# Attention and a 4-bit feed-forward pass on one core: another share-out of the decode, the weight sums and the row transfers in the down pass

## The chip, the cores and the metric

One core of one Trainium2 chip. The metric is the device time of one execution in microseconds (us), lower is better. TensorE (PE) multiplies, VectorE (DVE), ScalarE (ACT) and GpSimd (POOL) compute elementwise, SyncE (SP) and POOL issue DMAs here. Each engine runs its own instructions in program order and meets the others only at semaphores.

## The reference

Cross attention with a residual, then a gated feed-forward pass whose three weight matrices are stored as 4-bit codes with one scale for each block of 64.

```python
def reference(x, ctx, Wq, bq, Wk, bk, gate_q, gate_absmax, up_q, up_absmax, down_q, down_absmax):
    # x, ctx: (8, 256, 1024)   gate_q, up_q: (3584, 1024) int32 0..15   down_q: (1024, 3584)
    t = layernorm(x)
    Q = t @ Wq.T + bq;  K = ctx @ Wk.T + bk
    attn = softmax(Q @ K.T / sqrt(1024))
    x = x + attn @ ctx
    W = NF4_CODE[q].reshape(-1, 64) * absmax[:, None]      # for each of gate, up, down
    t = layernorm(x)
    h = silu(t @ Wg.T) * (t @ Wu.T)                        # (8, 256, 3584)
    return x + h @ Wd.T
```

## The kernel before, in words

2048 tokens go through attention, then through gate and up (a loop over slots) and through down (`DOWN_STEPS` = 98 steps). All products are made in f16 with each f32 operand split into a high and a low half (`PARTS`: high by high, high by low, low by high), and the 2 by 2 block products are made by a scheme with 7 products instead of 8 (`PRODUCTS`), which needs sums of blocks of the activations ("forms") and of the weights ("sums").

**Down pass on TensorE** (`tensor`, L1971). 7 groups of `CH_PAIRS` = 14 steps. A step m (group m // 14, c = m % 14) multiplies one pair of hidden chunks into all 8 PSUM banks, 3 matmuls of 128x512 for each bank: 24 matmuls. The banks hold a whole group; at the end of a group each bank j is emptied by VectorE (`keep_first` L2136 for group 0, `add_down` L2143 for the others) and the next group's first matmul in that bank waits for it (`s_yev`). Group 0, 1 and 2 multiply by the decoded weight quadrants 0, 1 and 2 as they are, step by step: step m needs decoded piece m. Group 3 multiplies by a difference of quadrants 3 and 0 ("sum" 0 to 13, one for each step), groups 4 to 6 by further sums 14 to 55.

**Decode.** Each of the 56 pieces of the down weights (128x512) comes from one unit: a DMA brings the codes (`load_unit`, ring of 3), ScalarE makes 10 squares (`square`, L236 and L240, into a ring of `SQ_RING` = 4 places `un.sq`), VectorE makes 5 steps (`factor`, L262 for the first, L249 for the other four, each reading one finished square and waiting for the step before it). Then ScalarE casts the high half (`piece_hi`, L287), VectorE subtracts for the low half (`piece_lo`, L294), and SP turns the piece with a DMA transpose into its place (`turn_piece`, L217; `halves` is a ring of 5). In program order ScalarE has `piece_hi` of unit v-1 behind the fifth square of unit v, VectorE has `piece_lo` of unit v-1 behind step 2 of unit v. So a unit is 11 ScalarE and 6 VectorE instructions.

**Order by plan.** `Plan` counts, before anything runs, how many decode instructions each of the two engines issues in each phase; a phase is one down step. `quota` gives at most 6 VectorE and 12 ScalarE instructions to a phase of the down pass, which comes out as one unit (6 and 11). In program order the VectorE phase m is: the last activation forms (in the first steps of group 0), `sum_lo` of the phase before, the decode instructions, `sum_of`, in two steps of groups 2, 3 and 5 `with_first` (L2129, adds group 0's kept product to the rows; 8 in all), and at c = 13 the 8 evictions. Nothing else ties these phases to TensorE's steps: an eviction comes when VectorE has gone through everything ahead of it.

**Sums** (`sum_of` L2113, L2115, L2117, `sum_hi` L2027, `sum_lo` L2123). Three VectorE operations, one ScalarE cast, one VectorE subtraction, each waiting for the one before. `SUM_AT` puts sum 0 at phase 39 and then one in each phase to 52, and sums 14 to 55 at 54 to 95.

**Queues.** SP has the transposes and, at the end, the last 8 output stores. POOL has, in each step, the stores of forms, the loads of codes due in this phase, the load of the hidden activations for step m+6 (`load_h`, L1865, waits until TensorE is done with step m), and spread over four steps each the row stores of the group before (`store_y`, c 1 to 4) and the row loads of this group (`load_y`, c 6 to 9), 256 KB each, 8 in a group.

```python
            if m - 1 in SUM_AT:
                sum_lo(SUM_AT.index(m - 1))
            streams.dve.run(DOWN_PHASE + m)
            if m in SUM_AT:
                sum_of(SUM_AT.index(m))
```

## Time and profile before

| | |
|---|---|
| median of three runs | 2038.51 us (2037.82 to 2042.64) |
| profiled execution | 2047.5 us, of it the span from first to last instruction 2045.7 us |
| mean granted TensorE clock | 0.983 |
| busy: PE, DVE, ACT, POOL | 95%, 80%, 75%, 22% |
| down pass on TensorE (L1971) | first matmul 1470.8 us, last group ends at 2041.9 us |
| its matmuls | 2352, most 379 ns long, one begun every 0.216 us |

Times in rows are microseconds from the start of the span. A busy share is over the whole span and mixes stages; TensorE is busy nearly all the time in the gate and up stage and stands still now and then in the first half of the down pass. A row of the timeline is a run of like instructions: its start, its length, how many, and in brackets how long the engine had stood still before it and what ended that. Length is from the start of the first to the end of the last; instructions of one engine overlap a little, so that the distance of two starts is less than the length of one.

### The profile page before, as it was taken

The numbers are of one execution on the slowest core, as the hardware profiler recorded it, in microseconds if no ns is written. First come the engines' busy times: TensorE is split into PE (matmuls) and PEld (weight loads), VectorE is DVE, ScalarE is ACT, GpSimd is POOL, SyncE is SP. The second block draws the span as 40 slices with busy tenths as digits, with TensorE's granted clock in tenths as the row PEclk, the third lists the DMA queues.
The fourth block names the chain that finished last, engine by engine and source line by source line (L and its number), as shares of the span: only waits on it lengthen the run. The fifth ranks groups of instructions, "written<-read, shape, count | busy, mean of one in ns | idle before, by whom it ended". The sixth has DMA issues, their size and how long they took to land.

```text
span 2045.7 us, 29927 instructions
## 1 busy us (share of the span) xinstructions
PE 1944.8 (95%) x9872; PEld 985.3 (48%) x9872; DVE 1638.0 (80%) x2716; ACT 1541.9 (75%) x2856; POOL 455.5 (22%) x688
## 2 busy tenths in 40 slices
PE   8989999989999999999999999999997996899999
PEld 3468787744444444444444444444443442334444
DVE  7758798876988898898898889888877778885763
ACT  3768876847989988988998998897999997821110
POOL 0013633630111111121111111112232332212221
PEclk9999999989999999999999999999998998999999
DMA  9012787673644655455564645556596887745544
GB/s 338 25 42 78 206 225 195 174 279 77 154 125 114 139 133 131 120 142 126 123 155 114 135 129 134 129 124 139 162 236 170 226 209 187 201 129 175 165 147 142
DMA packets 387850, 314.63 MB, mean 154 GB/s; under 512 B 327280, under 2 KB 327280, under 8 KB 385776
## 3 DMA queue, kind: packets, MB, share of 16 engines
q1 hardware_dynamic: 334544, 136.00, 30.9%
q0 software_dynamic: 51072, 176.72, 26.4%
q8 instruction: 78, 1.28, 0.3%
q14 instruction: 76, 0.62, 0.1%
q10 hardware_dynamic: 2080, 0.01, 0.1%
HBM read 154.31 MB, written 82.31 MB: 116 GB/s over the span
## 4 chain that ended last, share of the span: by engine, by line
PE 34%; ACT 29%; DVE 20%; issue 11%; DVEq 0%; POOL 0%; ACTq 0%
PE ps L1929 18%; ACT sq L240 11%; PE ps L1971 10%; ACT sq L236 9%; DVE w L249 4%; ACT halves L287 3%; DVE tail L2096 2%; PE ps L1336 2%; ACT tail L2002 2%; PE ps L1297 2%; DVE halves L294 1%; ACT tail L2017 1%; DVE tail L2062 1%; DVE ps L2052 1%; PE ps L1273 1%
## 5 line engine op out<-in xcount | busy, mean ns | idle before, releaser
L1929 PE MATMUL ps<-T,wS 128*128 128x512 f16 x4704 | 1019.9, 379 | 10.5 <-ACT ps L1986 6.3
L1929 PEld LDWEIGHTS ps<-T,wS 128*128 128x128 f16 x4704 | 458.5, 98 | 568.5 <-issue 15.4
L249 DVE SCALAR_TENSOR_TENSOR w<-sq,w 128x512 f32<-128x512 f32 x672 | 477.3, 710 | 127.8 <-ACT sq L240 115.1
L240 ACT ACTIVATE sq<-sq 128x512 f32<-128x512 f32 x1008 | 572.0, 624 | 0.0
L236 ACT ACTIVATE sq<-q 128x512 f32<-128x512 int32 x672 | 409.4, 629 | 55.5 <-DVE w L249 54.4
L1971 PE MATMUL ps<-T,tail 128*128 128x512 f16 x1584 | 351.1, 383 | 42.0 <-DVE tail L2143 20.0
L1971 PEld LDWEIGHTS ps<-T,tail 128*128 128x128 f16 x1584 | 155.3, 99 | 235.3 <-issue 40.8
L287 ACT CAST halves<-w 128x512 f16<-128x512 f32 x252 | 155.1, 616 | 79.9 <-DVE w L249 69.1
L1971 PE MATMUL ps<-T,wS 128*128 128x512 f16 x768 | 171.3, 383 | 11.5 <-DVE tail L2143 9.0
L1854 POOL DMA_DIRECT2D keep_h<-tail x196 | 106.7, 544 | 337.1 <-DVE tail L2096 334.7
L294 DVE SCALAR_TENSOR_TENSOR halves<-w,halves 128x512 f16<-128x512 f32 x252 | 172.5, 690 | 9.2 <-ACT halves L287 7.1
L1336 PE MATMUL ps<-T 128*128 128x256 f16 x1536 | 176.6, 275 | 3.3 <-DVE T L1561 3.3
L2027 ACT CAST T<-w 128x512 f16<-128x512 f32 x56 | 34.4, 615 | 184.5 <-DVE w L2117 184.5
L2096 DVE SCALAR_TENSOR_TENSOR tail<-tail 128x512 f16<-128x512 f32 x196 | 134.0, 684 | 35.2 <-ACT tail L2017 35.1
L1336 PEld LDWEIGHTS ps<-T 128*128 128x128 f16 x1536 | 151.1, 99 | 23.0 <-DVE T L1561 4.9
L1971 PEld LDWEIGHTS ps<-T,wS 128*128 128x128 f16 x768 | 75.5, 99 | 105.0 <-issue 11.9
L2017 ACT CAST tail<-tail 128x512 f16<-128x512 f32 x196 | 119.2, 610 | 0.2 <-DVE tail L2078 0.2
L200 POOL DMA_DIRECT2D q<-in_L_ffn_up_q x52 | 28.2, 542 | 329.9 <-DVE w L249 205.3
L2062 DVE SCALAR_TENSOR_TENSOR tail<-ps,up_out,tail 128x512 f32<-128x512 f32 x112 | 83.6, 746 | 5.2 <-PE ps L1929 4.1
L203 POOL DMA_DIRECT2D q<-in_L_ffn_down_q x56 | 42.7, 763 | 181.7 <-DVE w L249 109.2
L271 DVE TENSOR_TENSOR w<-w 128x512 f32<-128x512 f32 x112 | 77.8, 707 | 1.3
L1226 POOL TENSOR_TENSOR T<-tail,T 128x256 f16<-128x256 f32 x64 | 57.3, 907 | 95.9 <-ACT T L1464 60.4
(216 smaller groups left out, 1881.6 us busy)
## 6 DMA issues: line engine op xcount, KB each, us to landing
keep_h<-tail POOLq DMA_DIRECT2D x196, 256.0 KB, 2.9
tail<-keep_h POOLq DMA_DIRECT2D x66, 512.0 KB, 4.3
wS<-keep_h POOLq DMA_DIRECT2D x32, 512.0 KB, 4.4
q<-in_L_ffn_down_q POOLq DMA_DIRECT2D x56, 256.0 KB, 4.0
q<-in_L_ffn_up_q POOLq DMA_DIRECT2D x52, 256.0 KB, 2.9
q<-in_L_ffn_gate_q POOLq DMA_DIRECT2D x48, 256.0 KB, 3.1
keep_x<-T SPq DMA_DIRECT2D x38, 256.0 KB, 2.8
T<-in_x SPq DMA_DIRECT2D x9, 1024.0 KB, 5.5
```

What stands on the lines that cost most here:

```text
L236: nc.scalar.activation(place, un.q[:, ring, :], ACT.Square, bias=b, scale=a).then_inc(un.s_act, 1)
L240: nc.scalar.activation(place, place, ACT.Square, bias=b, scale=a).then_inc(un.s_act, 1)
L249: nc.vector.scalar_tensor_tensor(out=un.w[:, buf, :], in0=un.sq[:, (i - 1) % SQ_RING, :], scalar=FACTORS[i - 1][1], in1=un.w[:, buf, :], o ...
L287: nc.scalar.copy(un.halves[:, z % HALF_RING, 0, :], un.w[:, buf, :]).then_inc(un.s_whi, 1)
L294: nc.vector.scalar_tensor_tensor(out=un.halves[:, z % HALF_RING, 1, :], in0=un.w[:, buf, :], scalar=1.0, in1=un.halves[:, z % HALF_RING, 0 ...
L1336: last = nc.tensor.matmul(r_bank(o), t.A[:, a, k, o * P:(o + 1) * P], xnT[:, c, k, :], start=k == 0 and j == 0, stop=k == KT - 1 and j == ...
L1854: nc.gpsimd.dma_start(t.hs[form, pair, :, side, :], t.hst[:, n % HST_RING].rearrange("p a d -> p (a d)")).then_inc(s_hst[n % HST_RING], 16)
L1929: last = nc.tensor.matmul(ps[:, bank, :], un.wS[:, z % SLOTS, a, kt, :], t.Tp[side][product][:, :, b, kt, :], start=fresh and n == 0, stop ...
L1971: last = nc.tensor.matmul(ps[:, j, :], h[:, j // PAIRS, a, tok], quad(q, c)[:, b].rearrange("p k d -> p (k d)"), start=fresh and n == 0, s ...
L2017: nc.scalar.copy(t.hst[:, n % HST_RING, 0, :], t.act_buf[2 * FORM_BUF[form] + side]).then_inc(s_hhi, 1)
L2062: nc.vector.scalar_tensor_tensor(out=t.act_buf[e], in0=ps[:, EVICT_BANK[product] + side, :], scalar=t.up_out[:, chunk:chunk + 1], in1=t.ac ...
L2096: nc.vector.scalar_tensor_tensor(out=t.hst[:, n % HST_RING, 1, :], in0=t.act_buf[2 * FORM_BUF[form] + side], scalar=1.0, in1=t.hst[:, n % ...
```

## The change

It does seven things, all in the down pass.

- **Quotas.** A phase has at most 6 VectorE and 10 ScalarE decode instructions in the first 42 steps, 9 and 16 after them. Decode so ends in phase 49 (before: 50).
- **Squares.** Six places (`DOWN_SQ_RING`) in place of four; the two new ones are free buffers of `un.w`. ScalarE can be up to six factors ahead of VectorE.
- **High halves.** One piece in three (piece 2, 5, 8, ...: 18 of 56) has its high half cast by VectorE (`piece_hi_dve`, behind step 1 of the next unit) and not by ScalarE.
- **Sums.** All five operations of a sum stand together on VectorE; the cast is now `nc.vector.tensor_copy`. They come three decode instructions ahead of the phase's end (`run(..., 3)`). `SUM_AT` is 41, 42, 43, 43, 44, 45, 45, 46, 47, 48, 48, 49, 50, 50 for sums 0 to 13, the rest as before. They use two temporary buffers, before four.
- **Rows.** `load_y` and `store_y` go from POOL to SP, all 8 at a time: stores of group g-1 at c = 0 of group g, loads at c = 2.
- **Codes.** POOL runs the loads of codes and the form stores two phases ahead (`Q_AHEAD`).
- **First product.** `with_first` runs in groups 4, 5 and 6, before in 2, 3 and 5; the signs follow.

By the plan, from eviction to eviction: between those of groups 0 and 1, ScalarE has 140 decode instructions (before 154); between those of groups 1 and 2, 142 (before 154), the last three of them squares of unit 45 behind sum 0; ahead of those of group 0 it has 17 fewer. VectorE has 84 from eviction to eviction in both. After the evictions of group 2 VectorE has 68 decode instructions and sums 1 to 13 left (before 50 and sums 3 to 13, and the last step of sum 2). A piece is turned three phases ahead of its use up to phase 19, two from 21 and one at 40 and 41 (before: four throughout).

```diff
-FRESH_GROUPS, WITH_FIRST, KEPT_GROUPS, MINUS_ROWS = (0, 2, 3), (2, 3, 5), (2, 3), (3, 6)
+FRESH_GROUPS, WITH_FIRST, KEPT_GROUPS, MINUS_ROWS = (0, 2, 3), (4, 5, 6), (2, 3), (3,)
+DOWN_SQ_RING = 6
+def high_on_dve(z):
+    return z >= GATE_UP_PIECES and (z - GATE_UP_PIECES) % 3 == 2
+def square_place(un, u, f):
+    n = (NF * (u - GATE_UP_UNITS) + f) % DOWN_SQ_RING
+    if u < GATE_UP_UNITS:
+        return un.sq[:, f % SQ_RING, :]
+    return un.sq[:, n, :] if n < SQ_RING else un.w[:, SUM_3 + n - SQ_RING, :]
+def piece_hi_dve(nc, dve, un, z):
+    v = z - GATE_UP_PIECES
+    dve.wait_ge(un.s_fac, STEPS * (GATE_UP_UNITS + v + 1))
+    dve.wait_ge(un.s_turned[z % HALF_RING], 16 * (z // HALF_RING))
+    nc.vector.tensor_copy(un.halves[:, z % HALF_RING, 0, :], un.w[:, v % 4, :]).then_inc(un.s_dhi, 1)
...
@@ decode_dve
             yield factor(nc, dve, un, t, GATE_UP_UNITS + v, i)
+            if i == 1 and v > 0 and high_on_dve(GATE_UP_PIECES + v - 1):
+                yield piece_hi_dve(nc, dve, un, GATE_UP_PIECES + v - 1)
             if i == 2 and v > 0:
                 yield piece_lo(nc, dve, un, GATE_UP_PIECES + v - 1)
@@ quota
-        return 6, 12
+        return (6, 10) if phase - DOWN_PHASE < 3 * CH_PAIRS else (9, 16)
@@ sum_steps
-            due = sum(done < piece for done in self.dve) - DOWN_PHASE + 2
-            steps.append(max(due, steps[-1] + 1 if steps else CH_PAIRS))
+            due = sum(done < piece for done in self.dve) - DOWN_PHASE + 1
+            steps.append(due)
@@ sync
         for m in range(DOWN_STEPS):
+            group, c = m // CH_PAIRS, m % CH_PAIRS
             turns_due(DOWN_PHASE + m)
...
+            if group > 1 and c == 0:
+                for j in range(BANKS):
+                    store_y(group - 1, j)
+            if group > 0 and c == 2:
...
+                for j in range(BANKS):
+                    load_y(group, j)
@@ gpsimd
-            if group == 0:
-                stores_due(SLOT_COUNT + m)
-            loads_due(DOWN_PHASE + m)
+            for ahead in range(Q_AHEAD + 1) if m == 0 else (Q_AHEAD,):
+                if m + ahead < CH_PAIRS:
+                    stores_due(SLOT_COUNT + m + ahead)
+                loads_due(DOWN_PHASE + m + ahead)
             load_h(m + H_RING)
-            if 1 <= c <= 4 and group > 1:
...
-                load_y(group, 2 * c - 12)
-                load_y(group, 2 * c - 11)
@@ scalar
-            if m in SUM_AT:
-                sum_hi(SUM_AT.index(m))
@@ sum_of
+            wait(dve, s_wsumlo, n - 1)
             nc.vector.tensor_tensor(tmp, left[:, 0], right[:, 0], ALU.subtract).then_inc(s_wdif, 1)
             ...
+            nc.vector.tensor_copy(place[:, 0], tmp).then_inc(s_wsumhi, 1)
             dve.wait_ge(s_wsumhi, n + 1)
+            nc.vector.tensor_tensor(place[:, 1], tmp, place[:, 0], ALU.subtract).then_inc(s_wsumlo, 1)
@@ vector
-            if m - 1 in SUM_AT:
-                sum_lo(SUM_AT.index(m - 1))
+            streams.dve.run(DOWN_PHASE + m, 3)
+            for n in sums_at(m):
+                sum_of(n)
             streams.dve.run(DOWN_PHASE + m)
-            if m in SUM_AT:
-                sum_of(SUM_AT.index(m))
```

## Rows read from the trace of the kernel before

**Rows 1.** The chain that ended last, 1470 to 1830 us: shares by line.

```profile
by line: ACT sq L240 32.5%; ACT sq L236 26.0%; issue 13.5%; ACT halves L287 7.7%; DVE w L249 2.8%; DVE tail L2129 1.9%; DVE tail L2143 1.9%; ACT T L2027 1.9%; DVE w L2115 1.8%; DVE w L2113 1.7%; PE ps L1971 1.6%; ACT tail L2017 1.1%; DVE ta
```

**Rows 2.** Busy time by stage: start:end, length, each engine's busy us (instructions), clock, DMA share, GB/s.

```profile
1473.30:1557.15 83.85, 71.40 (x330) 32.22 (x330) 64.97 (x101) 82.53 (x160) 24.59 (x41) 0.94 0.89 235
1557.15:1640.40 83.25, 74.29 (x336) 33.17 (x336) 61.47 (x93) 80.16 (x155) 22.44 (x36) 0.95 0.78 202
1640.40:1733.60 93.20, 75.29 (x336) 33.42 (x336) 73.91 (x112) 83.41 (x161) 27.59 (x45) 0.90 0.82 204
1733.60:1818.10 84.50, 73.40 (x318) 31.45 (x319) 72.29 (x111) 51.61 (x97) 19.33 (x34) 0.95 0.63 171
1824.40:2041.90 217.50, 217.50 (x1008) 98.13 (x1008) 132.06 (x199) 24.70 (x40) 45.23 (x84) 1.00 0.46 152
...
1480.00:1500.00 20.00, 20.00 (x94) 9.10 (x93) 16.50 (x27) 20.00 (x40) 7.40 (x12) 1.00 1.08 281
```

**Rows 3.** TensorE timeline in the down pass: start, length, instruction, count, idle before.

```profile
1534.38 10.52 PE L1971 MATMUL ps<-T,tail 128*128 128x512 f16 x48
...
1558.02 12.13 PE L1971 MATMUL ps<-T,tail 128*128 128x512 f16 x48 [13.12 <-DVE tail L2136]
...
1641.33 13.13 PE L1971 MATMUL ps<-T,wS 128*128 128x512 f16 x48 [9.02 <-DVE tail L2143]
...
1734.57 22.96 PE L1971 MATMUL ps<-T,tail 128*128 128x512 f16 x96 [17.95 <-DVE tail L2143]
...
1811.83 10.52 PE L1971 MATMUL ps<-T,tail 128*128 128x512 f16 x48
...
1824.38 10.52 PE L1971 MATMUL ps<-T,tail 128*128 128x512 f16 x48 [2.02 <-DVE tail L2143]
```

**Rows 4.** VectorE timeline: the evictions of groups 0 to 3 (same columns).

```profile
1557.19 4.86 DVE L2136 COPY tail<-ps 128x512 f32<-128x512 f32 x8
...
1640.44 4.04 DVE L2143 SCALAR_TENSOR_TENSOR tail<-ps,y_out,tail 128x512 f32<-128x512 f32 x6
...
1733.68 4.04 DVE L2143 SCALAR_TENSOR_TENSOR tail<-ps,y_out,tail 128x512 f32<-128x512 f32 x6
...
1823.49 4.04 DVE L2143 SCALAR_TENSOR_TENSOR tail<-ps,y_out,tail 128x512 f32<-128x512 f32 x6
```

**Rows 5.** ScalarE timeline behind the evictions of group 0.

```profile
1562.68 0.62 ACT L287 CAST halves<-w 128x512 f16<-128x512 f32 x1 [3.09 <-DVE w L249]
```

**Rows 6.** ScalarE by line, 1473.3 to 1557.15 us: the casts of forms.

```profile
L2017 ACT CAST tail<-tail 128x512 f16<-128x512 f32 x9 | 5.4, 605 | 0.0
```

**Rows 7.** VectorE timeline: part of one unit with nothing to wait for.

```profile
1562.57 0.68 DVE L262 SCALAR_TENSOR_TENSOR w<-q,sd 128x512 f32<-128x512 int32 x1
1563.29 1.42 DVE L249 SCALAR_TENSOR_TENSOR w<-sq,w 128x512 f32<-128x512 f32 x2
1564.62 0.68 DVE L294 SCALAR_TENSOR_TENSOR halves<-w,halves 128x512 f16<-128x512 f32 x1
```

**Rows 8.** VectorE timeline: end of one sum, and four `with_first` in group 2.

```profile
1760.52 0.69 DVE L2117 TENSOR_TENSOR w<-w,T 128x512 f32<-128x512 f32 x1
...
1762.03 0.69 DVE L2123 TENSOR_TENSOR T<-w,T 128x512 f16<-128x512 f32 x1 [0.81 <-ACT T L2027]
...
1762.63 0.68 DVE L249 SCALAR_TENSOR_TENSOR w<-sq,w 128x512 f32<-128x512 f32 x1
...
1714.79 2.73 DVE L2129 SCALAR_TENSOR_TENSOR tail<-tail,y_out 128x512 f32<-128x512 f32 x4
```

**Rows 9.** VectorE by line and shape: one tensor input against two, 1024 wide.

```profile
L858 DVE TENSOR_SCALAR wS<-T,bqk 128x1024 f32<-128x1024 f32 x2 | 1.5, 752 | 0.0
L860 DVE SCALAR_TENSOR_TENSOR wS<-T,bqk,wS 128x1024 f32<-128x1024 f32 x10 | 12.8, 1282 | 0.2
```

**Rows 10.** DMA issues, KB each, us to landing: last stores by SP; transposes in group 0.

```profile
out<-tail SPq DMA_DIRECT2D x6, 256.0 KB, 2.1
T<-halves SPq DMA_TRANSPOSE x15, 3.6
```

More of the change, by code:

```diff
@@ L130, in unit_place, with highs_on @@
     return 2 * pair + (quad in (1, 2)), 2, quad // 2, v % 4
+def high_on_dve(z):
+    return z >= GATE_UP_PIECES and (z - GATE_UP_PIECES) % 3 == 2
+def highs_on(dve, z):
+    return sum(high_on_dve(n) == dve for n in range(z + 1))
 def last_piece_in(buf, before):
@@ L374, in dve_unit @@
                 fac[u, i] = d
+                if i == 1 and copied is not None and high_on_dve(copied):
+                    d += 1
                 for z in late.get(i, ()):
@@ L500, in __init__, with run @@
         self.steps, self.upto, self.done = steps, upto, 0
-    def run(self, phase):
-        while self.done < self.upto[phase]:
+    def run(self, phase, short=0):
+        while self.done < self.upto[phase] - short:
             next(self.steps)
```

122 lines of the change are left out of this document (66 added, 56 removed).

## The prediction

> **What bounds the kernel now.** I read first where TensorE stands still in the down pass [rows 3]. Forty-eight matmuls take 10.36 us start to start, so a step of 24 is 5.18 us and the 98 steps want 507.6 us; they take 571.1 (1470.8 to 2041.9). The loss of 63 us lies wholly in the first half. At the end of group 0 (1544.9) TensorE waits 13.1 us for VectorE's first eviction, after group 1 it waits 9.0, after group 2 18.0. Behind each of these waits the next 48 matmuls take 12.1 or 13.1 us in place of 10.4: the granted clock fell to its lower level, 1.2 GHz, while the engine stood. Within group 3 it loses 15 us: from 1734.57 to its last step, the second half of the row at 1811.83, so 1817.0, are 82.4 us for 13 steps of 5.18 (67.3). Groups 4 to 6 run without a gap, 217.5 busy of 217.5 [rows 2].
>
> Then I ask what the late eviction was waiting for. It is ready to go at the front of VectorE's queue only at 1557.19, 1640.44 and 1733.68 [rows 4], and TensorE goes on 0.85 us after each. In groups 0 and 1 VectorE is busy 65 of 84 and 61 of 83 us, ScalarE 82.5 and 80.2 [rows 2]: ScalarE is full, and two thirds of the chain are its squares and casts [rows 1]. 160 instructions in 82.53 us are 0.52 us each. A unit has 11 of them, so 5.7 us against TensorE's 5.18, and that is how VectorE, which waits for the squares, falls behind. From eviction to eviction the sum closes: 154 x 0.52 = 80.1, and one wait of 3.1 us in which ScalarE's cast stands behind VectorE's evictions [rows 5], makes 83.2; the rows of 4 are 83.25 apart. In group 3 it turns round: VectorE 72 busy of 84.5, ScalarE 52 [rows 2]. There VectorE is the bound.
>
> **The change, part by part.** I follow VectorE's first eviction of each group, called E0 to E3, since TensorE resumes 0.85 us behind it.
>
> *To E0.* The plan wants 17 fewer ScalarE instructions ahead of it: 17 x 0.52 = 8.8 us. The forms' casts stay [rows 6]. The two more places for squares let ScalarE come up to four instructions further before the pass begins; from none to four, I take two, 1.0 us. E0 = 1557.2 - 8.8 - 1.0 = 1547.4. VectorE would allow it: 65 us of work in 74. TensorE resumes at 1548.3, a wait of 3.4 us, not 13.1.
>
> *E0 to E1.* 140 ScalarE instructions, 72.8 us. Six places don't help against the wait of rows 5, because it is a cast and not a square: the cast of piece 18 stands six instructions (3.1 us) behind the one that E0 needed and wants a VectorE step that comes 5.5 us after E0; 2.4 us. VectorE's own last steps ahead of the eviction add 0.7. E1 = 1623.3. At E1 the next such cast is 15 instructions away, so there it costs nothing.
>
> *E1 to E2.* 139 instructions to the last square ahead of sum 0, 72.3 us; then a step, sum 0, two steps and a cast stand ahead of the eviction on VectorE. Starts are 0.72 us apart where one instruction needs the one before, 0.60 where not [rows 7]. A sum was 3 x 0.72, then a wait for ScalarE's cast, 1.5 us from L2117 to L2123, then 0.60 [rows 8]. Now the cast is VectorE's own. The trace has no cast from SBUF to SBUF of this size on VectorE. A 1024-wide operation with one tensor input takes 752 ns, one with two 1282 [rows 9], and two inputs at 512 0.68 to 0.69 us [rows 7, 8]. So I bound it by 0.38 (half of 752 ns) and 0.69 us. Two inputs at 512 and 1024 wide leave a fixed part of 2 x 0.69 - 1.28 = 0.10 us; with it the nearest row gives (0.75 - 0.10) / 2 + 0.10 = 0.425 us, and I take 0.42; a sum is 3 x 0.72 + 0.45 + 0.60 = 3.2. These steps make 5.5 us. E2 = 1623.3 + 77.8 = 1701.1, where it was 1733.7: 32.6 us won. The 8 `with_first` that have left group 2 (0.66 each, 5.3 us [rows 8]) are in that, since they stand nowhere in the chain of the new E2.
>
> The page "VectorE: DVE Perf Modes" of the Trainium skill, section "The perf-mode tier table", says that an f32 `tensor_copy` within SBUF runs at twice the rate of a two-input operation; the trace agrees as far as it goes (752 against 1282 ns). An estimate from its 1227 ns for 2048 elements, a quarter of it, is 0.31 us; with that the sum would move by under 2 us.
>
> *Group 3.* Here the change puts work onto the engine that is the bound. After E2 VectorE has 8 evictions (8 x 0.66 = 5.3), 68 decode instructions and 13 sums, where it had 50 and 11. I went through its program order with 0.72 and 0.60. Sum 9 is the last that TensorE waits for, in step 51: 60 decode instructions at 0.63 and 9 sums at 3.2 end 66.7 us after the evictions, so step 51 begins at E2 + 72.2. On the way TensorE waits 6.5 us for sum 1 (it stands behind the 8 evictions and 6 decode instructions), then some 4, 1.5, 4, 1.5, 4 and 3.5: 25 us, where it now waits 15. ScalarE has 115 instructions for the same stretch, 60 us, and hides. Its casts of pieces stay coupled to VectorE's steps; where no sum lies between this costs about 0.2 us a unit, 1.5 in all. From step 51 TensorE runs by itself, and sums 14 and 15 are done 1.7 us before they would hold up E3. Group 4 begins at E2 + 72.2 + 5 x 5.18 + 1.5 = E2 + 99.6 = 1800.7. It was 1824.4: 23.7 us won. With the copy at 0.38 or 0.69 this moves by -1 or +3. A fall of the clock costs nothing while VectorE or ScalarE sets the next wait; behind step 51 it would cost up to 1.8 us (12.13 against 10.36 [rows 3]).
>
> *Behind it.* Sums at 3.2 us stay under a step of 5.18; with two steps of four `with_first` (2.7 each) and 8 evictions group 5 or 6 is 14 x 3.2 + 5.3 + 5.3 = 55 us of 72.5. Nothing there stops TensorE now and nothing will. The tail behind the last matmul is the same.
>
> *Queues.* POOL loses the 8 + 8 row transfers of a group and takes code loads two phases early. Such a load waits for ScalarE and VectorE, and behind it in POOL's queue stands the load of activations for step m+6; it is held up to about step m+2 and lands 5 us later, two steps in hand: nothing. SP takes the rows: 8 at once, 2 MB, in the queue of the transposes. At the end of the pass the last stores land 2.1 us after issue with nothing beside them [rows 10] and keep up with one eviction each 0.66 us; in the groups the engines are 0.8 to 0.9 busy [rows 2], so I give a burst 5 to 17 us, taken as 10. Stores wait for VectorE's evictions, with the next transposes behind them, which wait for later VectorE work anyway. Worst placed are the loads at c = 2 of group 2: the transpose of piece 33 is issued at about E1 + 18, behind loads issued from E1 + 13 to 17, lands (3.6 us alone [rows 10]) at E1 + 25, and step 33 wants it at E1 + 26.7. I charge 1 us; between 0 and 7 for this burst.
>
> The sum: 23.7 - 1.0 = 22.7 us. The profiled execution would go from 2047.5 to 2024.8; it lies 9 us above the median of the runs, and the same gain there gives 2038.5 - 22.7 = **2015.8 us**.
>
> **Rivals.**
> - *More, ScalarE further ahead* (chance 0.13): all four instructions at E0, no cast wait behind it, sum 0 hidden because VectorE catches up behind its evictions (its units are 4.1 us against 5.2). For it: 61 busy of 83. Against: sum 0 stands behind the last squares. 1 + 2.4 + 3.3 more: 29 to 35 won, 2004 to 2010.
> - *Transfers in bursts hold the transposes* (0.15): each of the bursts in groups 2 and 3 costs TensorE or VectorE's sums 3 to 6 us, four bursts: 5 to 13 us won, 2026 to 2034. For it: a lead of one or two steps where there were four, and a DMA share of 0.82 over 93 us in group 2 that becomes 0.98 if the same work is done in 78. Against: 20 us at 281 GB/s and a share of 1.08 are in the rows too, and 204 x 93/78 = 243 is wanted [rows 2].
> - *The engines don't gain from pacing and places* (0.05): only the casts leave ScalarE, nine or ten before E1 at 0.52, and group 3 loses 10: some 10 won, 2028.
> - *Slower* (0.04): the same bursts, but at every one of five (c = 2 of group 1 too) VectorE itself stops for a transpose, and ScalarE behind it. It decides from 4.7 us a burst on (23.7 / 5); at 6 us the result is 2045. The page "DMA: Bandwidth & Descriptors" of the Trainium skill, section "Queues, rings and completion order", speaks for it: descriptors of one queue are consumed in ring order, so that a transpose issued by SP can't pass its row transfers. No row here shows a transpose behind 2 MB.
>
> **How the numbers follow.** The forecast (0.63) is VectorE-bound group 3 with E2 some 30 us earlier, 2009 to 2024. With the first rival and most of the second the range is 2004 to 2031. A measurement can tell about 0.3%, 6 us: faster 0.93, same 0.03, slower 0.04.
>
> **What would show it.** First evictions near 1547, 1623 and 1701; TensorE waits of about 3, 2 and 5 us at the ends of groups 0 to 2; ScalarE full in groups 0 to 2, VectorE full and waiting for nothing in group 3, where TensorE waits for L2123's successor, the sum's last subtraction, longest at step 43; no gap from group 4 on. The cast on VectorE at 0.38 to 0.45 us. The prediction is wrong if TensorE waits for transposes in group 2, if VectorE waits for them in its sums, or if E0 stays above 1552.

## The result, and the profile after

| | before | after |
|---|---|---|
| median of 20 runs each, side by side | 2042.70 us | 2029.38 us |
| ratio, 95% interval | | 0.9941 [0.9928, 0.9954] |
| profiled execution, its span | 2047.5, 2045.7 us | 2032.0, 2030.2 us |
| mean granted TensorE clock | 0.983 | 0.986 |
| down pass, first matmul to last | 571.1 us | 563.0 us |

The kernel is 12 us faster (0.0059 x 2042.7, between 9 and 15), where 22.7 were forecast. The time is inside the range, and the forecast gain is nearly double the measured one. That E2 came at 1701.0 us where 1701.1 was forecast is luck: the pass of this profile began 7.4 us earlier than that of the kernel before (1463.4 against 1470.8), so places are compared below by their distances.

Below, "distances" are those of the prediction: from the first matmul of the pass to E0, E0 to E1, E1 to E2, and E2 to the start of group 4.

| us | to E0 | E0-E1 | E1-E2 | E2-group 4 | pass |
|---|---|---|---|---|---|
| before | 86.4 | 83.2 | 93.2 | 90.8 | 571.1 |
| forecast | 76.6 | 75.9 | 77.8 | 99.6 | 547.4 |
| after | 78.8 | 76.8 | 81.9 | 107.9 | 563.0 |

The forecast's pass is 571.1 less the 23.7 us of its sum. Two different things stand in the difference of 15.6 us: 3.1 at the first two evictions, and 12.4 in groups 2 and 3.

VectorE's timeline of the changed kernel, the first evictions of groups 0, 1 and 2 (compare rows 4):

```profile
1542.23 4.87 DVE L2185 COPY tail<-ps 128x512 f32<-128x512 f32 x8
...
1619.06 4.04 DVE L2192 SCALAR_TENSOR_TENSOR tail<-ps,y_out,tail 128x512 f32<-128x512 f32 x6
...
1701.00 4.04 DVE L2192 SCALAR_TENSOR_TENSOR tail<-ps,y_out,tail 128x512 f32<-128x512 f32 x6
```

TensorE's timeline of the changed kernel (compare rows 3): the pass's first matmuls, and its longer stops.

```profile
1463.41 1.46 PE L2032 MATMUL ps<-T,tail 128*128 128x512 f16 x6
...
1543.07 12.44 PE L2032 MATMUL ps<-T,tail 128*128 128x512 f16 x48 [5.43 <-DVE tail L2185]
...
1619.95 10.52 PE L2032 MATMUL ps<-T,wS 128*128 128x512 f16 x48 [2.29 <-DVE tail L2192]
...
1651.55 7.64 PE L2032 MATMUL ps<-T,tail 128*128 128x512 f16 x24 [5.53 <-DMA T<-halves]
...
1701.89 5.34 PE L2032 MATMUL ps<-T,tail 128*128 128x512 f16 x24 [1.26 <-DVE tail L2192]
1713.58 7.35 PE L2032 MATMUL ps<-T,tail 128*128 128x512 f16 x24 [6.35 <-DVE T L2173]
...
1765.70 6.89 PE L2032 MATMUL ps<-T,tail 128*128 128x512 f16 x24 [4.00 <-DVE T L2173]
1780.03 8.25 PE L2032 MATMUL ps<-T,tail 128*128 128x512 f16 x24 [7.43 <-DVE T L2173]
```

Busy time by stage of the changed kernel (compare rows 2; columns: start:end, length, busy us and instructions of PE, PEld, DVE, ACT, POOL, then clock, DMA share, GB/s):

```profile
1466.30:1542.20 75.90, 71.34 (x330) 32.15 (x330) 63.00 (x100) 74.05 (x143) 21.98 (x36) 0.99 0.92 227
1542.20:1619.00 76.80, 74.60 (x336) 33.32 (x336) 59.24 (x93) 73.70 (x143) 18.45 (x29) 0.97 0.88 216
1619.00:1701.00 82.00, 75.14 (x336) 32.90 (x336) 62.62 (x99) 77.08 (x149) 17.82 (x29) 0.96 0.97 234
1701.00:1785.00 84.00, 57.94 (x228) 23.32 (x229) 75.47 (x122) 53.91 (x103) 11.18 (x18) 0.86 0.71 169
1808.80:2026.40 217.60, 217.60 (x1009) 98.54 (x1007) 157.32 (x251) 0.00 (x0) 19.91 (x37) 1.00 0.44 150
```

The share-out works as designed: ScalarE is full in groups 0 to 2 with 143, 143 and 149 instructions where it had 160, 155 and 161, and from group 4 on TensorE runs without a stop, 217.6 of 217.6. But in group 3, where VectorE should be busy throughout, it is busy 75.5 of 84.0. There it waits once, ahead of sum 9. VectorE's timeline of the changed kernel (L2162 to L2173 are the five operations of a sum):

```profile
1770.36 0.68 DVE L283 SCALAR_TENSOR_TENSOR w<-sq,w 128x512 f32<-128x512 f32 x1
1776.57 0.69 DVE L2162 TENSOR_TENSOR w<-T 128x512 f32<-128x512 f16 x1 [5.52 <-issue]
1777.30 0.69 DVE L2164 TENSOR_TENSOR w<-w,T 128x512 f32<-128x512 f32 x1
1778.02 0.69 DVE L2166 TENSOR_TENSOR w<-w,T 128x512 f32<-128x512 f32 x1
1778.82 0.43 DVE L2171 CAST T<-w 128x512 f16<-128x512 f32 x1
1779.28 0.69 DVE L2173 TENSOR_TENSOR T<-w,T 128x512 f16<-128x512 f32 x1
```

"issue" names no releaser; the operation reads `T`, which transposes fill, and the transposes issued in this stretch are very late. DMA issues of the changed kernel, 1755 to 1780 us (KB each, median us to landing):

```profile
tail<-keep_h POOLq DMA_DIRECT2D x4, 512.0 KB, 11.0
wS<-keep_h POOLq DMA_DIRECT2D x2, 512.0 KB, 10.5
...
T<-halves SPq DMA_TRANSPOSE x3, 11.6
```

A transpose took 3.6 us before [rows 10]. Beside it lie six loads of activations of 512 KB. Why they come together stands in POOL's timeline of the changed kernel (L215 loads codes, L1950 activations):

```profile
1742.61 0.55 POOL L1950 DMA_DIRECT2D tail<-keep_h  x1
1750.11 0.76 POOL L215 DMA_DIRECT2D q<-in_L_ffn_down_q  x1 [6.95 <-ACT w L274]
1757.61 0.75 POOL L215 DMA_DIRECT2D q<-in_L_ffn_down_q  x1 [6.75 <-ACT sq L270]
1758.35 0.55 POOL L1950 DMA_DIRECT2D tail<-keep_h  x1
1758.89 1.08 POOL L1950 DMA_DIRECT2D wS<-keep_h  x2
1761.63 1.06 POOL L1950 DMA_DIRECT2D tail<-keep_h  x2 [1.66 <-issue]
```

POOL stands twice for 7 us at a load of codes, until the decode has done with the buffer. No activations are loaded from 1743 to 1758, then five loads, 2.5 MB, are issued within 5 us.

The other place is group 2. There ScalarE waits for codes, 1.76 us and a little later, as below, 2.35 us; ScalarE's timeline, then the DMA issues of 1625 to 1662 us, where SyncE's eight row loads went out from 1633.2 to 1637.8:

```profile
1655.99 1.15 ACT L270 ACTIVATE sq<-q 128x512 f32<-128x512 int32 x2 [2.35 <-DMA q<-in_L_ffn_down_q]
```

```profile
tail<-keep_y SPq DMA_DIRECT2D x6, 256.0 KB, 5.7
...
q<-in_L_ffn_down_q POOLq DMA_DIRECT2D x5, 256.0 KB, 6.3
...
T<-halves SPq DMA_TRANSPOSE x7, 7.7
```

The two waits of ScalarE, 1.76 + 2.35 = 4.1, are the 4.1 us by which E1 to E2 misses the forecast. TensorE's 5.5 us stop for a transpose at 1651.55 costs nothing of its own: VectorE is late anyway, and TensorE's stop at the end of the group is only 1.3.

So the theory so far: the engines' arithmetic of the forecast holds to 3 us, and 12 us are lost to transfers that collide, 4 in group 2 behind the row burst and 8 in group 3 behind the piled-up activation loads.

### The profile page after: what moved, and what is told of

Its sections match the earlier page's. It is cut to its first block, busy times and chain, and to the rows that moved or that the text cites. A ratio compares the mean times of both kernels' runs of the same rounds, so it can differ in the third digit from the quotient of the medians.

```text
span 2030.2 us, 29928 instructions
## 1 busy us (share of the span) xinstructions
PE 1947.2 (96%) x9872; PEld 985.3 (49%) x9872; DVE 1658.9 (82%) x2790; ACT 1499.9 (74%) x2782; POOL 410.7 (20%) x600
## 4 chain that ended last, share of the span: by engine, by line
PE 37%; ACT 25%; DVE 20%; issue 10%; DMA 2%; POOL 0%; DVEq 0%; ACTq 0%; SPq 0%
PE ps L1990 18%; PE ps L2032 14%; ACT sq L274 8%; ACT sq L270 6%; DVE w L283 4%; DVE tail L2145 2%; ACT halves L321 2%; ACT tail L2063 2%; PE ps L1399 2%; DVE halves L339 2%; ACT tail L2078 1%; PE ps L1360 1%; DMA T<-halves 1%; ACT w L274 1%; DVE tail L2111 1%
## 5 line engine op out<-in xcount | busy, mean ns | idle before, releaser
L274 ACT ACTIVATE sq<-sq 128x512 f32<-128x512 f32 x898 | 514.0, 632 | 0.0
L283 DVE SCALAR_TENSOR_TENSOR w<-sq,w 128x512 f32<-128x512 f32 x598 | 423.4, 708 | 96.3 <-ACT sq L274 86.0
L270 ACT ACTIVATE sq<-q 128x512 f32<-128x512 int32 x598 | 366.3, 636 | 56.1 <-DVE w L283 52.8
L2032 PE MATMUL ps<-T,tail 128*128 128x512 f16 x1584 | 356.6, 387 | 33.4 <-DVE T L2173 19.8
L321 ACT CAST halves<-w 128x512 f16<-128x512 f32 x234 | 145.3, 621 | 88.1 <-DVE w L283 77.3
L215 POOL DMA_DIRECT2D q<-in_L_ffn_down_q x56 | 42.9, 766 | 249.9 <-ACT sq L274 83.0
L2063 ACT ACTIVATE tail<-ps,gate_out 128x512 f32<-128x512 f32 x112 | 76.1, 682 | 3.3 <-PE ps L1990 2.6
```

What stands on the lines that cost most here:

```text
L270: nc.scalar.activation(place, un.q[:, ring, :], ACT.Square, bias=b, scale=a).then_inc(un.s_act, 1)
L274: nc.scalar.activation(place, place, ACT.Square, bias=b, scale=a).then_inc(un.s_act, 1)
L283: nc.vector.scalar_tensor_tensor(out=un.w[:, buf, :], in0=square_place(un, u, i - 1), scalar=FACTORS[i - 1][1], in1=un.w[:, buf, :], op0=A ...
L321: nc.scalar.copy(un.halves[:, z % HALF_RING, 0, :], un.w[:, buf, :]).then_inc(un.s_whi, 1)
L2032: last = nc.tensor.matmul(ps[:, j, :], h[:, j // PAIRS, a, tok], quad(q, c)[:, b].rearrange("p k d -> p (k d)"), start=fresh and n == 0, s ...
L2063: nc.scalar.activation(t.act_buf[e], ps[:, EVICT_BANK[product] + side, :], ACT.Silu, scale=t.gate_out[:, 2 * pair + row:2 * pair + row + 1 ...
```

## The experiments

### Which transfers: rows spread, codes on time, rows back in POOL's queue

`u1_rows_spread` is the changed kernel with SyncE's row transfers two per step:

```diff
-            if group > 1 and c == 0:
-                for j in range(BANKS):
-                    store_y(group - 1, j)
-            if group > 0 and c == 2:
...
-                for j in range(BANKS):
-                    load_y(group, j)
+            if 1 <= c <= 4 and group > 1:      # two stores
+            if 6 <= c <= 9 and group > 0:      # two loads
```

> The changed kernel, but SP moves the rows two at a time, stores at c = 1 to 4 and loads at c = 6 to 9 of a group, as the kernel before had them. Theory BURST (the 8 row loads at once delay codes and transposes in group 2): ScalarE's two waits for codes there (1.8 and 2.4 us) and TensorE's 5.5 us wait for a transpose go, E1 to E2 is 78 us and not 82, some 3 to 5 us faster than the changed kernel, ratio to the kernel before 0.992. The 5.5 us wait of VectorE ahead of sum 9 stays. Theory CODES (the code loads two phases early hold back the activation loads behind them in POOL's queue, which then come in a burst): E1 to E2 stays at 82.

Measured: 2028.25 us, ratio 0.9927 [0.9902, 0.9953]; distances 78.8, 76.8, **77.6**, 107.7; pass 558.3. The 4.3 us of group 2 are gone. VectorE still waits 5.6 us ahead of sum 9, with transposes at 11.9 us. By this run the bursts bear on group 2 and not on group 3; whether they do each time is looked at below.

`u3_codes_on_time` is the changed kernel with codes loaded in the phase in which they are due:

```diff
-    Q_AHEAD = 2
+    Q_AHEAD = 0
```

> The changed kernel, but Q_AHEAD = 0: POOL issues the code loads and form stores of a phase in that step. Theory CODES: the six activation loads that stand together near the end of group 3 spread out, VectorE's 5.5 us wait ahead of sum 9 goes and with it 3 us of lower clock at step 51: E2 to the start of group 4 is 100 us and not 108, ratio 0.990. Theory BURST says that wait is not tied to the codes: 108 stays. The rival of both: code loads come later and ScalarE waits for them, slower than the changed kernel, ratio 0.996 or more.

Measured: 2032.10 us, ratio 0.9931 [0.9905, 0.9957]; distances 78.9, 79.5, 89.0, **100.5**; pass 565.3. In group 3 the wait at sum 9 is gone and transposes land in 3.2 us (three loads of activations are issued from 1755 to 1780 us, not six). But in group 2 both engines now stand for codes, VectorE 10.2 us and ScalarE as its timeline shows:

```profile
1658.18 1.15 ACT L270 ACTIVATE w<-q 128x512 f32<-128x512 int32 x2 [11.19 <-DMA q<-in_L_ffn_down_q]
```

Codes ahead are needed in group 2 and, with the rows on SyncE, harmful in group 3. One profile is one execution: here the pass is 5.8 us shorter than before, while the timed gain is 9 to 19 us, so the wait of group 2 is probably not always that long.

`u4_spread_and_on_time` has both edits of the diffs above.

> Both of the edits before together. If both theories hold, each for its own stretch, 12 us faster than the changed kernel: E1 to E2 78 us, E2 to group 4 100 us, ratio 0.988. If only one holds, as that one alone.

Measured: 2028.33 us, ratio 0.9923 [0.9896, 0.9950]; distances 78.9, 76.9, 87.8, 100.6; pass 561.7. Group 3 is as expected, group 2 is 10 us longer than the 78 expected. ScalarE waits 6.1, 1.4 and 1.5 us for codes there though the rows are spread, so with codes on time their lateness is that of POOL's queue, not of the burst.

`u2_rows_pool` is the changed kernel with the row transfers back in POOL's queue as in the kernel before, codes two phases ahead.

```diff
-            sp.dma_start(t.y_out_rows[j], t.ys[:, tile, cols])       # eight at c == 2
+            nc.gpsimd.dma_start(t.y_out_rows[j], t.ys[:, tile, cols]) # two at each c from 6 to 9
```

> The changed kernel, but the rows are back in POOL's queue (stores at c 1 to 4, loads at c 6 to 9), codes two phases early as changed. If the queue and not the burst mattered (transposes behind rows in one queue), it is as fast as the spread rows on SP or faster, ratio 0.990 to 0.992; if POOL's queue is the tight one (codes and activations behind the rows), slower than the changed kernel, ratio 0.996 or more.

Measured: 2024.17 us, ratio 0.9898 [0.9877, 0.9919]; distances 78.9, 76.9, 77.7, 100.6; **pass 551.6**. The last two distances are those of the arithmetic, the first two those of the changed kernel. In group 3 the activation loads now have row transfers between them in one queue. Transposes land in 7.7 us from 1755 to 1780 us, and VectorE waits for one only once, 0.4 us. That is close to the edge: two near copies below (`v3_quota12`, `v1_four_squares`) wait 1.4 and 1.8 us and have 101.7 and 102.6.

`b1_rows_sp` is the kernel *before* with only the row bursts by SyncE.

```diff
-                load_y(group, 2 * c - 12)       # POOL, c from 6 to 9
-                load_y(group, 2 * c - 11)
+                for j in range(BANKS):          # SyncE, c == 2; stores likewise at c == 0
+                    load_y(group, j)
```

> The kernel before, and of the whole change only the rows: by SP, eight stores at c = 0 and eight loads at c = 2. There a piece is turned four phases ahead and codes are loaded on time. If a burst costs only where the lead is short: within 2 us of the kernel before in every stretch (86.4, 83.2, 93.2, 90.8). If a burst of 2 MB delays codes whatever the lead: ScalarE waits for codes behind the row loads of groups 1 to 3, E1 to E2 3 to 10 us longer.

Measured, in one execution: 2040.88 us beside 2041.96 for the kernel before; distances 86.4, 83.2, 93.2, 90.8, pass 571.1, each as before. Transposes beside the burst of group 2 land in 5.2 us there, and with a lead of four phases the distances don't change.

`x5_spread_late` keeps the changed kernel's queues and takes both causes away: rows two per step as in the first experiment, and codes ahead only where they help.

```diff
             for ahead in range(Q_AHEAD + 1) if m == 0 else (Q_AHEAD,):
...
-                loads_due(DOWN_PHASE + m + ahead)
+                if m + ahead < 3 * CH_PAIRS:
+                    loads_due(DOWN_PHASE + m + ahead)
+            if m >= 3 * CH_PAIRS:
+                loads_due(DOWN_PHASE + m)
```

> The changed kernel with two edits: rows by SyncE two per step instead of eight at once, and codes fetched two phases ahead only in the first three groups, on time from the fourth on. My theory: the row bursts cost 4 us in group 2, and codes fetched ahead in group 3 hold the activation loads behind them, which makes the eight loads land together and the transposes late (7 us). So E1 to E2 77.6 us, E2 to the start of group 4 100.5, the pass 551 to 553 us, ratio to the kernel before 0.990. Rival, that VectorE's or TensorE's own work in group 3 is longer when SyncE carries the rows: E2 to group 4 stays at 107 to 108, the pass 558.

Measured: **2020.58 us**, ratio 0.9878 [0.9857, 0.9900]; distances 78.8, 76.8, 77.6, 100.3; pass 551.0. Its interval lies wholly below that of the changed kernel, and it beats both kernels; against `u2_rows_pool` the intervals overlap. Busy time of its groups 2 and 3, its DMA issues from 1745 to 1775 us, and TensorE at the place of the 7.43 us stop:

```profile
1620.70:1698.30 77.60, 72.68 (x336) 32.45 (x336) 62.38 (x98) 76.78 (x149) 18.24 (x29) 1.00 0.96 253
1698.30:1782.30 84.00, 66.36 (x266) 27.36 (x267) 80.72 (x131) 56.04 (x106) 11.64 (x18) 0.90 0.60 161
```

```profile
tail<-keep_h POOLq DMA_DIRECT2D x3, 512.0 KB, 5.7
...
T<-halves SPq DMA_TRANSPOSE x4, 3.1
```

```profile
1762.98 7.04 PE L2035 MATMUL ps<-T,tail 128*128 128x512 f16 x24 [3.99 <-DVE T L2176]
1771.68 5.35 PE L2035 MATMUL ps<-T,tail 128*128 128x512 f16 x24 [1.66 <-DVE T L2176]
```

VectorE is busy 80.7 of 84.0 in group 3, transposes land in 3.1 us, the long stop is 1.7 us. Group 2 moves its data at 253 GB/s with a DMA share of 0.96 and loses nothing: it is not the share that costs but who is late.

`x6_late` has the second edit alone, the bursts kept.

> The changed kernel with codes fetched on time from the fourth group on, the row bursts kept. Theory: E1 to E2 stays at 82 us (the burst's cost), E2 to the start of group 4 falls from 107.9 to 100.5 to 101.5, the pass 555 to 556 us. Rival, that the burst of group 3 is what delays the transposes there: E2 to group 4 stays at 106 or more.

Measured, in one execution: 2023.00 us; distances 78.8, 76.8, 81.7, 100.5; pass 555.2. The wait of group 3 goes with this edit alone. POOL still stands there for 7 us twice (6.96 and 6.75) at a load of codes; but two activation loads lie ready behind the second, and the next comes 3 us later, where five came in 5 us. So what went is the pile behind the hold and not the hold. That the pile slows the transposes of the other queue is read from their landing times, 11.6 to 12.5 us with it and 3.1 to 3.6 without.

`w1_swap` is `u2_rows_pool` with each step's activation load ahead of its load of codes, and `w2_ahead1` the same kernel with codes one phase ahead.

```diff
+            load_h(m + H_RING)                  # w1_swap: ahead of the loads of codes
             loads_due(DOWN_PHASE + m + ahead)
-            load_h(m + H_RING)
-    Q_AHEAD = 2                                 # w2_ahead1
+    Q_AHEAD = 1
```

> u2 (rows in POOL's queue), and in each step POOL issues the activation load for step m+6 first and the code load of two phases on after it. Theory HELD BACK (a code load that waits for the decode holds the activation loads behind it, which then come in a burst and slow the transposes that the sums wait for): the activation loads come one by one, no waits of VectorE for transposes in group 3, E2 to group 4 99 to 100 us where u2 had 100.6 and its near copies 101.7 and 102.6; ratio to the kernel before 0.989. Rival (the loads are in time anyway, contention is from the sum of bytes): 101 to 103.

> u2 with code loads one phase early in place of two. HELD BACK: the activation loads of group 3 come less bunched, 100 to 101 for E2 to group 4; ScalarE waits for codes at most 1 us in groups 1 and 2 (77, 78). If two phases are needed for the codes, ScalarE waits for them by 2 us or more in group 2.

Measured: `w1_swap` 2026.78 us, ratio 0.9929 [0.9907, 0.9951], distances 78.8, 76.8, 81.9, 103.4, pass 558.4. `w2_ahead1`, one execution: 2033.19 us, distances 78.8, 78.0, 79.5, 101.9, pass 555.6. Both lose in group 2, where codes come later. `w1_swap` was expected at 99 to 100 in group 3 and has 103.4, with one wait of VectorE for a transpose of 2.5 us; `w2_ahead1` has one of 1.7 us. So neither the order within a step nor one phase less keeps the transposes on time in this kernel, which had next to nothing to lose there. Whether they would help with the rows on SyncE was not tried.

### Do the two waits repeat?

`x1_again` and `b0_before_again` are the changed kernel and the kernel before once more, unaltered.

> The changed kernel once more, unaltered. Theory: the costs belong to its order of issue, so E1 to E2 is 81 to 83 us again and E2 to the start of group 4 106 to 109, the pass 562 to 564 us; the first two distances 78.8 and 76.8. Rival: both are accidents of one execution; then one of them is within 1 us of 77.6 or of 100.5.

> The kernel before once more, unaltered. Theory: the pass is 571.1 us again to within 0.5, and its beginning, 1470.8 in the first profile, varies with the execution: it lies between 1462 and 1468 here as in the other kernels. Rival: the change moved the beginning; then it is 1469 to 1472 again.

Measured: the changed kernel 2027.95 us, distances 78.8, 76.8, **77.6**, **106.9**, pass 557.5; the kernel before 2038.27 us, distances 86.4, 83.2, 93.2, 90.7, pass 571.1. TensorE and VectorE in the second execution of the changed kernel:

```profile
1648.63 5.35 PE L2032 MATMUL ps<-T,tail 128*128 128x512 f16 x24 [1.33 <-DMA T<-halves]
...
1776.79 7.35 PE L2032 MATMUL ps<-T,tail 128*128 128x512 f16 x24 [7.16 <-DVE T L2173]
```

```profile
1773.33 0.69 DVE L2162 TENSOR_TENSOR w<-T 128x512 f32<-128x512 f16 x1 [5.40 <-issue]
```

My theory was half wrong. The wait of group 3 is the kernel's own (5.52, 5.40, and 5.62 us with the rows spread). The 4.3 us of group 2 are not always there: 4.3 and 4.1 us were lost with the same burst in two executions and nothing in this one, with row loads and transposes landing about as late. So the burst as the cause of group 2 is likely and not shown: with it the distance was 81.9, 81.7 (`x6_late`) and 77.6, and without it and with codes two phases ahead 77.6 or 77.7 in `u1_rows_spread`, `u2_rows_pool`, `x5_spread_late` and `v3_quota12`; but `w1_swap` has 81.9 without a burst. A lead of two phases is on the edge. The pass is 8.1 us shorter than before in one execution and 13.6 in the other, and the timed gain of 12 lies between. The beginning of the pass, too, differs from one execution to the next: 1470.8 and 1461.6 us in two of the kernel before, 1460.9 to 1472.6 in the others. The 7.4 us by which the changed kernel's pass began earlier in its first profile are no gain of the change.

### The engines: places, pace, high parts, sums

All of these start from `u2_rows_pool` (pass 551.6; 78.9, 76.9, 77.7, 100.6), so that transfers hide little, and all but that base are single executions; the last distance of near copies differs by up to 2 us with a late transpose.

```diff
-DOWN_SQ_RING = 6                                            # v1_four_squares
+DOWN_SQ_RING = 4
-        return (6, 10) if phase - DOWN_PHASE < 3 * CH_PAIRS  # v3_quota12
+        return (6, 12) if phase - DOWN_PHASE < 3 * CH_PAIRS
-    return z >= GATE_UP_PIECES and (z - GATE_UP_PIECES) % 3 == 2  # v2_no_high
+    return False
```

> The changed kernel with the rows in POOL's queue (u2), and four places for squares in place of six. My step said that six places bring ScalarE up to four instructions ahead at E0 (1 us) and nothing elsewhere, since the wait behind the evictions is a cast's and not a square's: start to E0 some 1 us longer than in u2 (78.9), the rest as in u2 (76.9, 77.7, 100.6). The rival, that the places are what lets ScalarE run through the evictions: E0 to E1 and E1 to E2 longer by 2 us or more each.

Measured: 2021.63 us; 78.9, 76.8, 78.7, 102.6; pass 554.6. Two more places bring nothing at E0, where the forecast counted 1.0 us, and 1 us at E2; the 2.0 in group 3 hold a 1.8 us wait of VectorE for a transpose. So the whole pass is 3 us longer, of which a late transpose can be two thirds.

> u2, and 12 ScalarE instructions a phase in the first 42 steps in place of 10 (no pacing of ScalarE). ScalarE runs as fast as its operands let it either way, and VectorE's evictions need the same ScalarE instruction (1517, 1657, 1799): all four stretches within 0.5 us of u2's 78.9, 76.9, 77.7, 100.6. The rival, that pacing matters: start to E0 or E0 to E1 2 us longer or shorter.

Measured: 2030.43 us; 78.8, 76.8, 77.6, 101.7; pass 552.3. Raising ScalarE's quota changes each of the first three distances by 0.1 us at most. The last distance is 1.1 longer, not within the 0.5 expected, with a 1.4 us wait of VectorE for a transpose. By the plans of the two kernels VectorE has 84 decode instructions between evictions in both: its own quota of 6, which since the change also holds a cast for one unit in three, is what slows the decode. No run alters that quota.

> The changed kernel with rows back in GpSimd's queue (the fastest so far) and no high part of a square on VectorE: all of them on ScalarE again. One high part in three is some 40 instructions of 0.52 us of ScalarE's time over the pass, 5 per group. By the engine sums: S to E0 and E0 to E1 within 1 us of 78.8 and 76.8, since the decode, a planner's choice, moves back by 19 items; E1 to E2 77 to 79; E2 to group 4 100 to 104; the pass 552 to 556 against 551.6. Rival, that ScalarE ends the first groups: S to E0 longer by 2 us or more and the pass over 557.

Measured: 2032.87 us; 82.0, 74.5, 81.0, 106.5; pass 561.5. I expected at most 4 us and it is 10. My claim that the decode behind E0 would only move back was wrong: up to E0 ScalarE has 151 instructions in this kernel and 144 in `x5_spread_late`, and 7 x 0.52 = 3.6 us is what E0 loses, 3.2. In group 2 TensorE stands 5.1 us for a transpose. In group 3 the plan puts sum 10 a step later: it starts 79.6 us after E2, in `u2_rows_pool` 73.4, and it is the last one for which TensorE stops here, 3.9 us. The expectation's "some 40 instructions" was also wrong, since the change moves 18 casts. So one high part in three on VectorE is worth some 10 us here, 3 of them at E0.

`v4_sum_cut` and `v5_cast_act` alter the sum: the first leaves its third operation out, the second gives its cast back to ScalarE and puts three decode instructions of VectorE between the third operation and the last.

```diff
-            dve.wait_ge(s_wdif, 2 * n + 2)                   # v4_sum_cut
-            nc.vector.tensor_tensor(tmp, tmp, right[:, 1], ALU.subtract)
...
-            nc.vector.tensor_copy(place[:, 0], tmp)          # v5_cast_act
+            nc.scalar.copy(place[:, 0], un.w[:, W_TMP + n % 2, :])
```

> u2 with the last of the three operations of each weight sum left out (the low half of the right operand isn't subtracted, so the output differs a little): a sum is four VectorE instructions. If VectorE's own work bounds group 3, TensorE waits for sum 9 with nine sums 0.72 us shorter: E2 to group 4 6 to 7 us shorter than in u2 (100.6), 94; E1 to E2 0.7 shorter by sum 0. If ScalarE or a transfer bounds it: under 2 us.

Measured: 2019.49 us; 78.8, 76.8, 76.8, 100.8; pass 550.7. Up to sum 9 the expectation holds: step 51 begins 67.0 us after E2, in `u2_rows_pool` 73.6. But the distance to group 4 doesn't shorten. VectorE's timeline of this kernel says where the 6.6 us went:

```profile
1764.89 0.69 DVE L2168 TENSOR_TENSOR w<-T 128x512 f32<-128x512 f16 x1 [2.33 <-DMA T<-halves]
...
1779.88 0.69 DVE L2168 TENSOR_TENSOR w<-T 128x512 f32<-128x512 f16 x1 [3.77 <-DMA T<-halves]
...
1787.74 0.69 DVE L2168 TENSOR_TENSOR w<-T 128x512 f32<-128x512 f16 x1 [5.18 <-DMA T<-halves]
```

It waits 11.3 us for transposes, where `u2_rows_pool` waits 0.4. Behind VectorE the transposes are the next bound of group 3, 10.4 us each here.

> u2 with the cast of each sum back on ScalarE, and three decode instructions of VectorE between the sum's third operation and its last subtraction, so that VectorE doesn't wait for the cast. If VectorE's work is the bound and ScalarE has room (some 50 of 84 us busy): 9 x 0.45 = 4 us less for sum 9, less 2 us for its last subtraction coming later, E2 to group 4 98 to 99, 2 us shorter than u2. The rival, that the cast ties the two engines (ScalarE's squares stand behind a cast that waits for VectorE, which waits for the squares): 103 or more.

Measured: 2027.14 us; 78.8, 76.8, 76.9, 104.2; pass 554.1. With the cast on ScalarE, TensorE stops 7.3 us where it stopped 1.9. VectorE waits for ScalarE's cast, 2.5 us at the longest, and 2.7 us for a transpose. Moving the cast to VectorE is right even where VectorE is the bound: 3.6 us in group 3 and, since the variant gains 0.8 ahead of E2, 2.5 in the pass. The rival of the expectation, that the cast ties the two engines, is what came.

### The first product

`v6_first_early` is `u2_rows_pool` with `with_first` in groups 2, 3 and 5 again; `b2_first_late` is the kernel *before* with `with_first` in groups 4, 5 and 6, and nothing else.

```diff
-FRESH_GROUPS, WITH_FIRST, KEPT_GROUPS, MINUS_ROWS = (0, 2, 3), (4, 5, 6), (2, 3), (3,)
+FRESH_GROUPS, WITH_FIRST, KEPT_GROUPS, MINUS_ROWS = (0, 2, 3), (2, 3, 5), (2, 3), (3, 6)
...
```

> u2 with the kept first product added in groups 2, 3 and 5, as before, and not in 4, 5 and 6. By my step the eight operations in group 2 cost nothing where ScalarE bounds, except those that stand behind its last squares (steps 39 and 40 of 42): 0 to 3 us in E1 to E2 (77.7), and those of group 3, behind sum 13, nothing. Rival, that VectorE's queue is tight there too: 5.3 us.

> The kernel before with one part of the change alone: the first product's rows are combined in groups 4, 5 and 6 instead of 2, 3 and 5. The forecast priced this step at nothing in groups 2 and 3, since ScalarE sets the end there. By that, the pass stays within 1 us of 571.1, E2 to group 4 within 1 us of 90.8. Rival, by the run that undid it: the eight combinations of a group delay VectorE's evictions and sums where they stand, so taking them out gives 3 to 8 us in the kernel before too, in E1 to E2 or E2 to group 4.

Measured: `v6_first_early` 2044.07 us; 78.8, 76.8, **84.2**, **111.6**; pass 568.9, that is 17.3 longer. `b2_first_late` 2038.64 us; 86.4, 83.2, 89.7, 88.6; pass 565.4, that is 5.7 shorter. VectorE's timeline of the first, in group 2 and late in group 3:

```profile
1693.08 2.74 DVE L2184 SCALAR_TENSOR_TENSOR tail<-tail,y_out 128x512 f32<-128x512 f32 x4 [4.71 <-DMA wS<-keep_y]
...
1799.90 0.69 DVE L2168 TENSOR_TENSOR w<-T 128x512 f32<-128x512 f16 x1 [4.71 <-DMA T<-halves]
1806.53 2.73 DVE L2184 SCALAR_TENSOR_TENSOR tail<-tail,y_out 128x512 f32<-128x512 f32 x4
```

For the first I had written 0 to 3 us in group 2 and nothing in group 3, and it is 17 in the two; for the second the forecast's price was nothing, and its rival of 3 to 8 us came. In group 2 VectorE waits 4.7 us for row loads, which `with_first` needs and which come late in a shortened group; in group 3 eight combinations (5.3 us) and a wait of 4.7 for a transpose are 10.0 of the 11.0. In the kernel before, the same move was worth 3.5 and 2.2. This part alone is about a quarter of what `x5_spread_late` gains in the pass (20.1), and without it the rest, as measured in one execution, has next to nothing left: 2.2 us of pass. Part of the 17 us is waits, 4.7 us for rows and 4.7 for a transpose.

## Why the prediction was right in its arithmetic and wrong in its sum

**To E0: 9.8 forecast, 7.6 measured.** The 17 instructions were 8.5 us of ScalarE's time (82.53 to 74.05), as forecast. The 1.0 us for two more places was nothing (`v1_four_squares`). The other 1.2 us has no row of its own; ScalarE's idle time in the stretch grew by 0.5.

**E0 to E1: 75.9 forecast, 76.8 measured.** The cast wait was right: 76.8 less 73.7 busy is 3.1, which I had as 2.4 + 0.7. ScalarE had 143 instructions in the window, not 140.

**E1 to E2: 77.8 forecast, 77.6 or 77.7 in four kernels with the rows spread and codes two ahead** (`u1_rows_spread`, `u2_rows_pool`, `x5_spread_late`, `v3_quota12`)**.** The changed kernel has 81.9 or 77.6, by the execution.

**Group 3: 99.6 forecast, 100.3 to 100.6 where no transpose is late.** VectorE's copy took what was taken for it. By form, VectorE, 1466 to 1790 us of the changed kernel (busy us, mean ns, idle before):

```profile
L329 DVE CAST halves<-w 128x512 f16<-128x512 f32 x17 | 7.1, 420 | 0.0
...
L2171 DVE CAST T<-w 128x512 f16<-128x512 f32 x12 | 5.1, 427 | 1.2
```

The forecast had 0.42. The Trainium skill, page "VectorE: DVE Perf Modes", section "The perf-mode tier table", has this copy at twice the rate of two inputs; the trace gives 0.42 against 0.69, 1.6 times. The estimate from its figure, a quarter of the time of four times the size, was 0.31 us; it leaves out the part of an instruction that doesn't grow with its size, which the estimate from the rows had in. A sum starts 3.3 us after the one before where they stand side by side, against 3.2.

**The step that failed is the one on POOL's queue.** The prediction followed the activation loads behind a load of codes, found that they land two steps before TensorE wants them, and wrote "nothing". That is true of their own user: TensorE never stopped for them. It did not ask what they collide with once released. Five of them together raised a transpose in *another* queue from 3.6 to 11.6 us, and VectorE, the bound of group 3, needed that transpose: 5.5 us of wait and, with the lower clock behind TensorE's 7.4 us stop, 6.6 to 7.6 us of pass. `x6_late` takes only this away and gets 7.4 us back; of all that was tried, this is what is shown best.

**The charge for the bursts was a size.** I charged 1 us, with 0 to 7 for this burst; it was 4.1 to 4.3 in two executions and 0 in one. The place was right, the loads at c = 2 of group 2. The transpose of piece 33 was later than reckoned, 5.5 us of stop where 1.7 us were in hand; but what set E2 was ScalarE's codes, 1.76 and 2.35 us, where I had looked at the transpose alone. The rule of the Trainium skill quoted in the prediction, ring order within SyncE's queue, costs nothing by itself while the lead is four phases (`b1_rows_sp`). The Trainium skill's section has the descriptors taken in ring order, but also lets a later one finish its write first, so the prediction's "can't pass" goes further than the page. In group 3 SyncE's queue held no row transfer when the transposes were late. What bears on that is another sentence of the Trainium skill's page "DMA: Bandwidth & Descriptors", same section "Queues, rings and completion order": each DMA engine takes turns between the queues it has work for. The trace agrees as far as it goes: 11.6 us in SyncE's queue beside POOL's loads.

The sum as it was: 23.7 - 3.6 for the engines' terms (20.1, which `x5_spread_late` shows), then - 6.6 to 7.6 in group 3 and - 0 to 4.3 in group 2 = 8 to 13.5 us.

**The rivals.** The one on bursts (5 to 13 us won, 0.15) has the amount and half the mechanism. ScalarE further ahead is refuted. "The engines don't gain" had its premise right, since neither the places nor ScalarE's quota move E0 or E1, and its price wrong: E1 came 14.0 us nearer to the pass's beginning, not 5. The slower one never came near: VectorE stopped for a transpose once in the first profile, not five times. Of the three signs of being wrong that I named, two came: VectorE waited for a transpose in its sums, and TensorE for one in group 2, which by itself cost nothing.

**With_first.** The distances of the forecast had the eight combinations of groups 2 and 3 rightly left out. A price of the move by itself was missing for group 3, and when I had to give one I said nothing where it is 5.7 in the kernel before, and 0 to 3 where it is 17.3 in `u2_rows_pool`.

## What to carry to other kernels

A transfer that is held up and then released isn't free because its own user has time: price what it lands beside, in every queue, and above all the short transfers on which the bounding engine counts. Fetching ahead in an in-order queue helps while its consumer is the bottleneck and hurts when the consumer slows and the queue waits with everything behind it; switch it by stage. When an engine becomes the bound of a stage, work taken off it can be worth more than its own time (17.3 us for 10.6 us of combinations in two groups) or next to nothing (6.6 us won up to sum 9 and lost again behind it), so undo each part from the finished kernel as well as adding it to the old one.

## What the runs showed of the hardware

A VectorE cast of 128x512 from f32 to f16 within SBUF takes 0.42 to 0.43 us, against 0.69 for a two-input operation of the same size. A transpose of `halves` landed after 3.1 to 3.6 us where loads came one by one beside it, after 6.8 and 7.7 beside a 2 MB burst of rows and after 11.6 and 12.5 beside 3 MB of activations, five of whose six loads were issued within 5 us. The same program lost 4.3 us in group 2 in one execution and nothing in the next.

The clock follows the stops in steps. Busy time by stage of the changed kernel, behind the 5.43 us stop, behind the 2.29 us stop, and behind the 7.43 us stop:

```profile
1543.10:1547.00 3.90, 3.90 (x10) 1.43 (x11) 3.90 (x7) 1.54 (x3) 0.69 (x2) 0.50 0.69 212
1547.00:1555.00 8.00, 8.00 (x39) 3.63 (x38) 7.36 (x12) 7.26 (x14) 1.29 (x2) 1.00 0.40 82
1620.00:1630.00 10.00, 10.00 (x47) 4.21 (x48) 9.89 (x17) 10.00 (x21) 1.28 (x2) 1.00 0.98 319
1780.10:1784.00 3.90, 3.90 (x10) 1.41 (x11) 3.69 (x7) 0.09 (x1) 0.00 (x0) 0.50 0.16 63
```

Behind stops of 5.4 and 7.4 us TensorE had 0.50, its 1.2 GHz level, for some microseconds; behind 2.3 us it kept 1.00, 2.4 GHz. (Stops of 2.34 and 2.35 us were followed by 24 matmuls in 5.35 us or in 7.04, in the kernel before and in `b2_first_late`, so this is not fixed.) So the shorter stops of the changed kernel can save more than their own length: 48 matmuls behind the stop at the end of group 1 take 10.5 us, where they took 13.1 [rows 3].
